# Wavelet mixing on Trainium2: the synthesis products in longer runs, and the last edge projected with its coefficients stationary

## The chip, the cores and the metric

The kernel runs on one core of a Trainium2 chip. The metric is the device time of one execution in microseconds (us); lower is better. "Before" is the kernel without the change.

## The reference, cut to what matters

```python
x: (8, 512, 207, 64) fp32               # batch, time, nodes, channels
sig = x.transpose(0, 2, 3, 1).reshape(-1, T)
a = sig; details = []
for _ in range(3):                       # 8-tap wavelet analysis along time
    a, d = _dwt(a); details.append(d)
coeffs = [a] + details[::-1]             # four components
enh = [c * w[i] for i, c in ...]         # a weight per component and channel
rec = enh[0]
for d in enh[1:]:
    rec = _idwt(rec[:, :d.shape[-1]], d)   # synthesis along time
xr = rec[:, :T].reshape(B, N, D, T).transpose(0, 3, 1, 2)
return x + xr @ proj_w.T + proj_b        # 64x64 projection of the channels
```

Analysis and synthesis are linear in time, so the kernel holds each as a small banded matrix, and it projects the channels between the two.

## The kernel before, in words

The time axis of 512 steps is cut into four windows of 128, and each window into two halves of 64 steps. Two nodes of 64 channels make a pair (128 columns of `x_sb`), four pairs make a group, and nine groups make a turn of the loop; 23 turns make 207 groups. One group is one period of the schedule. The first and last turns are written out, those between are a hardware loop. All order between engines is written by hand, with semaphores: a `wait_ge` on an engine holds everything that stands behind it on that engine.

TensorE (PE) does four kinds of work. All of it uses one half of the array's rows (64 partitions) per matmul, and two matmuls on the two halves run side by side:

- Analysis (line 433, called by `analyse_first` and `analyse_second`, L441 and L462): `x_sb` is stationary (64x128), the 84 columns of the analysis matrix move. Each pair has a first and a second piece of four matmuls. They write the two banks of `coefs_ps`; VectorE (DVE) multiplies them by the component weights into `coefs_sb` (`scale_pair`, L706). There is one `coefs_ps`, so the first piece of the next pair waits for that (`scaled`, L455). GpSimd (POOL) then adds 20 shared columns of the two halves of the time axis (`add_seam`, L364, semaphore `seamed`), which the projection of window 2 waits for.
- Projection (`project`, L487): a window's coefficients (64x128) are stationary, and the 64x64 projection weight moves. Windows go in the order 2, 3, 0, 1 (`ORDER`). Windows 2 and 0 share `proj_ps[0]`, windows 3 and 1 share `proj_ps[1]`. ScalarE (ACT) rounds the result to fp32r (`copy_high`, L634), and DVE takes the rest (`split_low`, L712); the bank is free after that (`lo_copied`).
- The tail (`project_tail`, L497): the 20 coefficient columns past the last window of time, the "last edge". Before, the weight is stationary and the coefficients move (4 pairs of 32 columns), so the result has channels on partitions. DVE turns it (`turn_tail`, L724, two transposes), ACT moves it in four pieces of 20x128 into `tail_row` (`move_tail`, L646) and rounds it into the stack (L654), and POOL takes the rest (`split_tail`, L368).
- Synthesis (L518, L520, L530, L532, and the edges L542, L544): 512 columns of fp32r move. A unit is two windows: LATE is windows 2 and 3, EARLY is windows 0 and 1. `synthesise_first` has three steps of two matmuls, `synthesise_second` three more steps and the edge step. Before, `synthesise_first` is issued as step 0, then a piece of analysis, then steps 1 and 2. DVE adds the result to `x_sb` (`add_window`, L733).

A matmul of four-byte floats shows as two records in the trace, an fp32r matmul as one. A group in TensorE's order is written in `turn_of` (L547): the two projections of windows 2 and 3 with two analysis pieces, the tail, the EARLY unit of the group two behind, then windows 0 and 1, then the LATE unit of the group one behind, and the first half of window 2 of the next group. DVE's order (`turn_of` there, its calls at the end of its block) is: add windows 2 and 3, scale pair 0, split 2, split 3, turn the tail, scale pair 1, add windows 0 and 1, scale pair 2, split 0, split 1, scale pair 3. POOL's (L393): seam 0, wait for window 3, seam 1, four DMAs, seam 2, split the tail, wait for window 1, seam 3, four DMAs. ACT's: copy 2, copy 3, an edge, move and round the tail, an edge, copy 0, copy 1, an edge. SP issues loads of `x` and stores of the output, paced by the count of analysed pairs.

Of the kernel before, what the change touches and what calls it, by code (L numbers as in the profile page):

```python
# [7 lines left out]
BATCH, TIME, NODES, CHANNELS = 8, 512, 207, 64  # L8
# [7 lines left out]
WINDOWS = TIME // WINDOW  # L16
# [8 lines left out]
QUAD = 32  # L25
# [5 lines left out]
TAIL_AT = PART_COLS + SEAM  # L31
PAIR_COLS = TAIL_AT + QUAD

# [106 lines left out]
def wavelet_mix(nc, x, comp_w, w_t, bias, analysis_m, synthesis_m, edge_m, out):  # L140
# [11 lines left out]
    with ExitStack() as ctx:  # L152
        def sb(name, shape, dtype=fp32):
            return ctx.enter_context(nc.sbuf_tensor(name, shape, dtype))
# [4 lines left out]
        def sem(name):  # L159
            return ctx.enter_context(nc.semaphore(name))  # L160
# [16 lines left out]
        bias_parts = sb("bias_parts", [1, BIAS_PARTS, GROUP], fp32r)  # L177
        coefs_sb = sb("coefs_sb", [PAIR, COEF_SETS * PAIRS, PAIR_COLS])
        proj_hi = [[sb(f"proj_hi{w}_{i}", [WINDOW, GROUP], fp32r) for i in range(SETS)] for w in range(WINDOWS)]
        proj_lo = [[sb(f"proj_lo{w}_{i}", [WINDOW, GROUP], fp32r) for i in range(SETS)] for w in range(WINDOWS)]  # L180
        tail_sb = sb("tail_sb", [4 * QUAD, PAIRS * QUAD])
        tail_row = sb("tail_row", [QUAD, GROUP])
# [31 lines left out]
        lo_copied = sem("lo_copied")  # L214
        turned = sem("turned")
        tail_moved = sem("tail_moved")
# [31 lines left out]
        def proj_of(w):  # L248
            return proj_ps[PLACE[w] % 2]
# [104 lines left out]
        def _(pool):  # L354
            nc.gpsimd.memset(stack_sb[:, EARLY * SETS:(EARLY + 1) * SETS, :].bitcast(fp32), 0.0).then_inc(stacks_cleared, 1)
            pool.wait_ge(comp_loaded, 2 * 16)
            build_scale(nc.gpsimd, 0).then_inc(scale_built, 1)

            def add_seam(turn, g, p):
                done = (turn * GROUPS + g) * PAIRS + p  # L360
                coefs = coefs_of(g, p)
                halo, own = coefs[:, SEAM:SEAM + HALO_COLS], coefs[:, PART_COLS:PART_COLS + HALO_COLS]
                pool.wait_ge(scaled, done + 1)
                nc.gpsimd.tensor_tensor(own, halo, own, ALU.add).then_inc(seamed, 1)  # L364

            def split_tail(turn, g):
# [54 lines left out]
        def _(pe):  # L421
# [49 lines left out]
            def project(turn, g, w, pairs, first):  # L471
                group = turn * GROUPS + g
                if pairs[0] == 0:
                    if w in UNITS[LATE]:
                        if not (first and g == 0):
                            pe.wait_ge(lo_copied, group * WINDOWS + (PLACE[w] - 1))
                    else:
                        pe.wait_ge(lo_copied, group * WINDOWS + (PLACE[w] - 1))
                        if w == ORDER[3]:
                            pe.wait_ge(turned, group + 1)  # L480
                for p in pairs:
# [10 lines left out]

            def project_tail(g):
                at = (g % COEF_SETS) * PAIRS
                for node in range(2):
                    rows = node_rows[node]
                    mm = nc.tensor.matmul(proj_of(ORDER[1])[:, node, NODE_COLS:NODE_COLS + PAIRS * QUAD], w_sb[rows, :],  # L497
                                          coefs_sb[rows, at:at + PAIRS, TAIL_AT:TAIL_AT + QUAD],
                                          start=True, stop=True, skip_group_check=True)
                mm.then_inc(projected, 1)  # L500
# [46 lines left out]
            def turn_of(turn, first=False, last=False):  # L547
                for g in range(GROUPS):
# [14 lines left out]

                    first_ahead(0)
                    project(turn, g, 2, [2, 3], first)
                    second_ahead(0)
                    project(turn, g, 3, [0, 1, 2, 3], first)
                    project_tail(g)
                    if with_early:
                        synthesise_first(*twice, EARLY, [0], False)  # L570
                    first_ahead(1)
                    if with_early:
                        synthesise_first(*twice, EARLY, [1, 2], False)
                    second_ahead(1)
                    if with_early:
                        synthesise_second(*twice, EARLY)
                    project(turn, g, 0, [0, 1], first)
                    first_ahead(2)
                    project(turn, g, 0, [2, 3], first)
                    second_ahead(2)  # L580
                    project(turn, g, 1, [0, 1, 2, 3], first)
                    if opening:
                        pe.wait_ge(lo_built, 2)
                        pe.wait_ge(stacks_set, 16 * STACK_DMAS)
                    if with_late:
                        synthesise_first(*behind, LATE, [0], opening)
                    first_ahead(3)
                    if with_late:
                        synthesise_first(*behind, LATE, [1, 2], opening)
                    second_ahead(3)  # L590
                    if with_late:
                        synthesise_second(*behind, LATE)
                    if not (last and g + 1 == GROUPS):
                        project(*ahead, 2, [0, 1], False)

# [4 lines left out]
            pe.wait_ge(scaled, PAIRS)  # L600
            project(0, 0, 2, [0, 1], True)
            turn_of(0, first=True)
# [8 lines left out]
        def _(act):  # L611
# [25 lines left out]
            def move_tail(turn, g, first):  # L637

                group = turn * GROUPS + g
                act.wait_ge(turned, group + 1)  # L640
                if not (first and g == 0):
                    act.wait_ge(tail_hi_copied, group)
                    act.wait_ge(tail_lo_copied, group)
                for q in range(4):
                    cols = slice(q * PAIRS * QUAD, (q + 1) * PAIRS * QUAD)
                    nc.scalar.activation(tail_row[0:HALO_COLS, cols], tail_sb[q * QUAD:q * QUAD + HALO_COLS, :],  # L646
                                         ACT.Copy).then_inc(tail_moved, 1)
# [36 lines left out]
        def _(dve):  # L684
            nc.vector.memset(warm_sb[:, :], 0.0).then_inc(warm_cleared, 1)
            nc.vector.memset(w_sb[:, :], 0.0).then_inc(cleared, 1)
            nc.vector.memset(coefs_sb[:, :, TAIL_AT + HALO_COLS:PAIR_COLS], 0.0)
            nc.vector.memset(stack_sb[:, LATE * SETS:(LATE + 1) * SETS, :].bitcast(fp32), 0.0).then_inc(stacks_cleared, 1)
# [27 lines left out]

            def turn_tail(turn, g, first):
                group = turn * GROUPS + g
                dve.wait_ge(projected, group * WINDOWS + 2)
                if not (first and g == 0):  # L720
                    dve.wait_ge(tail_moved, group * TAIL_MOVES)
                for node in range(2):
                    rows = node_rows[node]
                    last = nc.vector.transpose(tail_sb[rows, :],  # L724
                                               proj_of(ORDER[1])[rows, node, NODE_COLS:NODE_COLS + PAIRS * QUAD])
                last.then_inc(turned, 1)

            def add_window(turn, g, w):
# [6 lines left out]
            def turn_of(turn, first=False, last=False):  # L735
                for g in range(GROUPS):
# [14 lines left out]
                    split_low(turn, g, 3)  # L751
                    turn_tail(turn, g, first)
                    scale_ahead(1)
# [55 lines left out]
```

## Time and profile before

| | |
|---|---|
| median of 3 runs | 2275.58 us |
| lowest, highest | 2274.68, 2275.77 us |
| the profiled execution's own time | 2273.99 us |
| its span | 2272.1 us |
| busy share: PE, PE weight loads, DVE, ACT, POOL | 99, 95, 78, 55, 55 % |
| traffic of HBM over the span | 191 GB/s, DMA engines busy 60 to 70 % |
| groups | 207 |

The span is the stretch in which instructions ran in the profiled execution; the execution's own time is 1.9 us longer. The busy share of TensorE counts overlapping matmuls and modelled ends, so it does not say that the array works at its peak.

### The profile page before, as it was taken

The page shows a single profiled execution, that of the slowest core. Times are in us where ns is not written, and L with a number is a line of the kernel's source. Part 1 is how long each engine was busy: PE and PEld are TensorE (multiplying, and loading weights), DVE is VectorE, ACT ScalarE, POOL GpSimd, SP SyncE. Part 2 cuts the span into 40 slices and gives each one's busy share as a digit, 9 for nine tenths or more (in the row PEclk, how much of TensorE's full clock was granted, in tenths as well). Part 3 has the DMA queues.
Part 4 walks back from the last instruction along what each step waited for, and adds up shares of the span by engine and source line. Part 5 has one row for each costly group of instructions (what it writes and reads, how often), then busy time and mean ns, then how long its engine had stood idle before and what let it go on. Part 6 is the DMA issues. An engine that isn't in the chain of part 4 may idle for free.

```text
span 2272.1 us, 84681 instructions
## 1 busy us (share of the span) xinstructions
PE 2255.5 (99%) x33152; PEld 2155.0 (95%) x33152; DVE 1779.9 (78%) x2920; ACT 1248.6 (55%) x2489; POOL 1250.7 (55%) x2708
## 2 busy tenths in 40 slices
PE   9999999999999999999999999999999999999998
PEld 8999999999999999999999999999999999999997
DVE  4878777777777787777778777777777777777776
ACT  3555555555555555555555555555555555555554
POOL 3555555555555555555555555555555555555554
PEclk9999999999999999999999999999999999999999
DMA  4666767676676766767677676766767667676765
GB/s 144 211 212 217 245 213 254 210 240 222 210 250 214 249 209 215 250 210 252 208 232 234 204 255 208 249 213 214 249 210 249 213 219 241 210 256 207 247 218 174
DMA packets 165718, 507.53 MB, mean 223 GB/s; under 512 B 48710, under 2 KB 49990, under 8 KB 165403
## 3 DMA queue, kind: packets, MB, share of 16 engines
q1 hardware_dynamic: 111656, 434.23, 56.3%
q0 software_dynamic: 52992, 68.02, 12.1%
q8 instruction: 296, 4.85, 0.9%
q10 hardware_dynamic: 754, 0.28, 0.0%
q14 instruction: 20, 0.16, 0.0%
HBM read 217.33 MB, written 217.06 MB: 191 GB/s over the span
## 4 chain that ended last, share of the span: by engine, by line
PE 99%; issue 0%; DVE 0%; DMA 0%; ACT 0%; DVEq 0%; ACTq 0%
PE coefs_ps L433 33%; PE proj_ps L487 31%; PE synth_ps L518 11%; PE synth_ps L530 9%; PE synth_ps L532 4%; PE synth_ps L520 3%; PE synth_ps L542 3%; PE proj_ps L497 2%; PE synth_ps L544 1%; DVE x_sb L733 0%; DMA x_sb<-x 0%; PE proj_ps L433 0%; PE synth_ps L433 0%; DVE proj_lo L712 0%; ACT proj_hi L634 0%
## 5 line engine op out<-in xcount | busy, mean ns | idle before, releaser
L433 PE MATMUL coefs_ps<-analysis_sb,x_sb 64*128 64x84 f32 x13200 | 1029.0, 272 | 2.7 <-issue 1.9
L433 PEld LDWEIGHTS coefs_ps<-analysis_sb,x_sb 64*128 64x128 f32 x13200 | 959.5, 188 | 48.2 <-issue 3.5
L634 ACT ACTIVATE proj_hi<-proj_ps 128x512 fp32r<-128x512 f32 x828 | 494.3, 597 | 796.9 <-PE proj_ps L487 568.6
L487 PE MATMUL proj_ps<-w_sb,coefs_sb 64*128 64x64 f32 x13248 | 928.4, 268 | 2.6 <-issue 2.6
L487 PEld LDWEIGHTS proj_ps<-w_sb,coefs_sb 64*128 64x128 f32 x13248 | 896.8, 189 | 28.3 <-issue 2.8
L706 DVE TENSOR_TENSOR coefs_sb<-coefs_ps,scale_sb 128x552 f32<-128x552 f32 x825 | 604.3, 733 | 285.1 <-PE coefs_ps L433 277.6
L364 POOL TENSOR_TENSOR coefs_sb<-coefs_sb 128x20 f32<-128x20 f32 x828 | 188.1, 227 | 961.5 <-DVE coefs_sb L706 958.5
L712 DVE TENSOR_TENSOR proj_lo<-proj_ps,proj_hi 128x512 fp32r<-128x512 f32 x828 | 560.4, 688 | 137.3 <-ACT proj_hi L634 111.2
L733 DVE TENSOR_TENSOR x_sb<-synth_ps,x_sb 128x512 f32<-128x512 f32 x828 | 531.2, 683 | 56.2 <-PE synth_ps L544 56.1
L664 ACT ACTIVATE stack_sb<-proj_hi 20x512 fp32r<-20x512 f32 x621 | 387.1, 623 | 11.6
L646 ACT ACTIVATE tail_row<-tail_sb 20x128 f32<-20x128 f32 x828 | 255.3, 308 | 179.8 <-DVE tail_sb L724 164.7
L384 POOL DMA_DIRECT2D stack_sb<-proj_hi x621 | 314.0, 506 | 33.4 <-issue 31.8
L384 POOL DMA_DIRECT2D stack_sb<-proj_lo x621 | 313.9, 505 | 0.0
L368 POOL TENSOR_TENSOR tail_lo<-tail_row,stack_sb 20x512 fp32r<-20x512 f32 x207 | 263.9, 1275 | 0.1
L518 PE MATMUL synth_ps<-proj_hi,synthesis_lo 64*128 64x512 f32 x414 | 197.6, 477 | 5.2 <-DVE x_sb L733 5.2
L520 PE MATMUL synth_ps<-proj_hi,synthesis_lo 64*128 64x512 f32 x414 | 197.8, 478 | 0.0
L530 PE MATMUL synth_ps<-proj_hi,synthesis_lo 64*128 64x512 f32 x414 | 197.0, 476 | 0.3
L532 PE MATMUL synth_ps<-proj_hi,synthesis_lo 64*128 64x512 f32 x414 | 197.0, 476 | 0.0
L518 PE MATMUL synth_ps<-proj_lo,synthesis_hi 64*128 64x512 f32 x414 | 196.7, 475 | 0.0
L520 PE MATMUL synth_ps<-proj_lo,synthesis_hi 64*128 64x512 f32 x414 | 196.4, 474 | 0.0
L542 PE MATMUL synth_ps<-stack_sb,edge_all 64*128 64x512 f32 x414 | 162.3, 392 | 0.0
L530 PE MATMUL synth_ps<-proj_hi,synthesis_hi 64*128 64x512 f32 x414 | 162.2, 392 | 0.0
(57 smaller groups left out, 2716.5 us busy)
## 6 DMA issues: line engine op xcount, KB each, us to landing
x_sb<-x SPq DMA_DIRECT2D x364, 576.0 KB, 4.5
out<-x_sb SPq DMA_DIRECT2D x364, 576.0 KB, 3.5
stack_sb<-proj_hi POOLq DMA_DIRECT2D x621, 40.0 KB, 2.2
stack_sb<-proj_lo POOLq DMA_DIRECT2D x621, 40.0 KB, 3.3
stack_sb<-stack_sb POOLq DMA_DIRECT2D x207, 40.0 KB, 2.2
stack_sb<-tail_lo POOLq DMA_DIRECT2D x207, 40.0 KB, 3.3
out<-x_sb SPq DMA_DIRECT2D x1, 1280.0 KB, 4.7
x_sb<-x SPq DMA_DIRECT2D x1, 1024.0 KB, 9.3
```

Source lines behind the costliest of these rows:

```text
L384: pool.dma_start(stack_of(g, u)[rows, :].bitcast(fp32), source[0:HALO_COLS, :].bitcast(fp32)).then_inc(sent, 16)
L433: return lambda cols: nc.tensor.matmul(out[:, at:at + HALF_COLS], x_sb[half_rows[side], w, cols], analysis_sb[half_rows[side], :], start=s ...
L487: mm = nc.tensor.matmul(out_cols[:, :, p, :], coefs_of(g, p)[rows, own_cols(w)], w_sb[rows, rows].rearrange("k (h c) -> k h c", h=2), star ...
L518: nc.tensor.matmul(synth_ps[0][:, :], weight[half_rows[0], :], low[half_rows[0], :], start=step == 0, stop=False, skip_group_check=True)
L520: mm = nc.tensor.matmul(synth_ps[1][:, :], weight[half_rows[1], :], high[half_rows[1], :], start=step == 0, stop=False, skip_group_check=True)
L530: nc.tensor.matmul(synth_ps[1][:, :], weight[half_rows[0], :], high[half_rows[0], :], start=False, stop=False, skip_group_check=True)
L532: nc.tensor.matmul(synth_ps[0][:, :], weight[half_rows[1], :], low[half_rows[1], :], start=False, stop=False, skip_group_check=True)
L634: nc.scalar.activation(proj_hi[w][g % SETS][:, :].rearrange("k (n c) -> k n c", n=2), proj_of(w)[:, :, 0:NODE_COLS], ACT.Copy).then_inc(hi ...
L664: nc.scalar.activation(stack_of(g, u)[rows, :], proj_hi[w][g % SETS][0:HALO_COLS, :].bitcast(fp32), ACT.Copy).then_inc(edge_moved[w], 1)
L706: nc.vector.tensor_tensor(coefs, banks[:, :, 0:PART_COLS], scale_sb[:, :, :], ALU.mult).then_inc(scaled, 1)
L712: nc.vector.tensor_tensor(proj_lo[w][g % SETS][:, :].rearrange(by_node, n=2), proj_of(w)[:, :, 0:NODE_COLS], proj_hi[w][g % SETS][:, :].bi ...
L733: nc.vector.tensor_tensor(cols, rec, cols, ALU.add).then_inc(summed, 1)
```

## The change: what it does

TensorE's order in a group is rewritten. `synthesise_first` is issued whole, for both units. The piece of analysis that stood inside it comes after it; then come two pairs of projection; then the second piece of analysis and `synthesise_second`. To have those pairs of projection there, windows are projected in other portions: window 2 as pairs 0 and 1, pair 2, pair 3; window 3 and window 1 as pair 0 and pairs 1 to 3; window 0 as pairs 0 and 1, pair 2, pair 3.

The tail is projected like a window: GpSimd copies its 20 columns of each pair, right after the seam, side by side into a new tile `tails_sb`, that tile is stationary, and the weight moves. The result then has time on partitions, and the two DVE transposes with `tail_sb` and the semaphore `turned` are gone. ACT moves it from PSUM (four pieces as before, one for each pair), and waits for DVE's split of window 3 before it does. TensorE waits for the tail's move before it projects window 1 into the same banks.

```diff
@@ GpSimd
             pool.wait_ge(comp_loaded, 2 * 16)
+            pool.wait_ge(tails_cleared, 1)
...
                 nc.gpsimd.tensor_tensor(own, halo, own, ALU.add).then_inc(seamed, 1)
+                nc.gpsimd.tensor_copy(tails_sb[:, g % COEF_SETS, p * QUAD:p * QUAD + HALO_COLS],
+                                      coefs[:, TAIL_AT:TAIL_AT + HALO_COLS]).then_inc(tailed, 1)
@@ TensorE
                         if w == ORDER[3]:
-                            pe.wait_ge(turned, group + 1)
+                            pe.wait_ge(tail_moved, (group + 1) * TAIL_MOVES)
...
-            def project_tail(g):
-                at = (g % COEF_SETS) * PAIRS
+            def project_tail(turn, g):
+
+                i = g % COEF_SETS
+                pe.wait_ge(tailed, (turn * GROUPS + g + 1) * PAIRS)
                 for node in range(2):
                     rows = node_rows[node]
-                    mm = nc.tensor.matmul(proj_of(ORDER[1])[:, node, NODE_COLS:NODE_COLS + PAIRS * QUAD], w_sb[rows, :],
-                                          coefs_sb[rows, at:at + PAIRS, TAIL_AT:TAIL_AT + QUAD],
+                    mm = nc.tensor.matmul(proj_of(ORDER[1])[:, node, NODE_COLS:NODE_COLS + CHANNELS],
+                                          tails_sb[rows, i, :], w_sb[rows, rows],
                                           start=True, stop=True, skip_group_check=True)
...
                     first_ahead(0)
-                    project(turn, g, 2, [2, 3], first)
+                    project(turn, g, 2, [3], first)
+                    project(turn, g, 3, [0], first)
                     second_ahead(0)
-                    project(turn, g, 3, [0, 1, 2, 3], first)
-                    project_tail(g)
+                    project(turn, g, 3, [1, 2, 3], first)
+                    project_tail(turn, g)
                     if with_early:
-                        synthesise_first(*twice, EARLY, [0], False)
+                        synthesise_first(*twice, EARLY, [0, 1, 2], False)
                     first_ahead(1)
-                    if with_early:
-                        synthesise_first(*twice, EARLY, [1, 2], False)
+                    project(turn, g, 0, [0, 1], first)
                     second_ahead(1)
                     if with_early:
                         synthesise_second(*twice, EARLY)
-                    project(turn, g, 0, [0, 1], first)
+                    project(turn, g, 0, [2], first)
                     first_ahead(2)
-                    project(turn, g, 0, [2, 3], first)
+                    project(turn, g, 0, [3], first)
+                    project(turn, g, 1, [0], first)
                     second_ahead(2)
-                    project(turn, g, 1, [0, 1, 2, 3], first)
+                    project(turn, g, 1, [1, 2, 3], first)
...
                     if with_late:
-                        synthesise_first(*behind, LATE, [0], opening)
+                        synthesise_first(*behind, LATE, [0, 1, 2], opening)
                     first_ahead(3)
-                    if with_late:
-                        synthesise_first(*behind, LATE, [1, 2], opening)
+                    if not (last and g + 1 == GROUPS):
+                        project(*ahead, 2, [0, 1], False)
                     second_ahead(3)
                     if with_late:
                         synthesise_second(*behind, LATE)
                     if not (last and g + 1 == GROUPS):
-                        project(*ahead, 2, [0, 1], False)
+                        project(*ahead, 2, [2], False)
@@ ScalarE, move_tail
-                act.wait_ge(turned, group + 1)
+                act.wait_ge(lo_copied, group * WINDOWS + (PLACE[ORDER[1]] + 1))
...
-                for q in range(4):
-                    cols = slice(q * PAIRS * QUAD, (q + 1) * PAIRS * QUAD)
-                    nc.scalar.activation(tail_row[0:HALO_COLS, cols], tail_sb[q * QUAD:q * QUAD + HALO_COLS, :],
+                by_pair = tail_row[0:HALO_COLS, :].rearrange("k (n h p c) -> k n h p c", n=2, h=2, p=PAIRS)
+                for p in range(PAIRS):
+                    tail = proj_of(ORDER[1])[p * QUAD:p * QUAD + HALO_COLS, :, NODE_COLS:NODE_COLS + CHANNELS]
+                    nc.scalar.activation(by_pair[:, :, :, p, :], tail.rearrange("k n (h c) -> k n h c", h=2),
                                          ACT.Copy).then_inc(tail_moved, 1)
@@ VectorE
-            nc.vector.memset(coefs_sb[:, :, TAIL_AT + HALO_COLS:PAIR_COLS], 0.0)
+            nc.vector.memset(tails_sb[:, :, :], 0.0).then_inc(tails_cleared, 1)
...
-            def turn_tail(turn, g, first):
-                group = turn * GROUPS + g
-                dve.wait_ge(projected, group * WINDOWS + 2)
-                if not (first and g == 0):
-                    dve.wait_ge(tail_moved, group * TAIL_MOVES)
-                for node in range(2):
-                    rows = node_rows[node]
-                    last = nc.vector.transpose(tail_sb[rows, :],
-                                               proj_of(ORDER[1])[rows, node, NODE_COLS:NODE_COLS + PAIRS * QUAD])
-                last.then_inc(turned, 1)
...
                     split_low(turn, g, 3)
-                    turn_tail(turn, g, first)
                     scale_ahead(1)
```

## Rows read from the trace of the kernel before

**Rows 1.** The page: span, busy time of each engine, granted clock.

```profile
span 2272.1 us, 84681 instructions
...
PE 2255.5 (99%) x33152; PEld 2155.0 (95%) x33152; DVE 1779.9 (78%) x2920; ACT 1248.6 (55%) x2489; POOL 1250.7 (55%) x2708
...
PEclk9999999999999999999999999999999999999999
```

**Rows 2.** The page: chain that ended last, by engine.

```profile
PE 99%; issue 0%; DVE 0%; DMA 0%; ACT 0%; DVEq 0%; ACTq 0%
```

**Rows 3.** Timeline of TensorE from 1006.41 us: start, duration, line, operation, records.

```profile
1006.41 0.55 PE L487 MATMUL proj_ps<-w_sb,coefs_sb 64*128 64x64 f32 x8
1006.80 0.63 PE L433 MATMUL coefs_ps<-analysis_sb,x_sb 64*128 64x84 f32 x8
1007.27 0.59 PE L487 MATMUL proj_ps<-w_sb,coefs_sb 64*128 64x64 f32 x8
1007.70 0.63 PE L433 MATMUL coefs_ps<-analysis_sb,x_sb 64*128 64x84 f32 x8
1008.16 1.04 PE L487 MATMUL proj_ps<-w_sb,coefs_sb 64*128 64x64 f32 x16
1009.04 0.44 PE L497 MATMUL proj_ps<-coefs_sb,w_sb 64*128 64x128 f32 x4
1009.23 0.48 PE L518 MATMUL synth_ps<-proj_hi,synthesis_lo 64*128 64x512 f32 x1
...
1009.55 0.57 PE L433 MATMUL coefs_ps<-analysis_sb,x_sb 64*128 64x84 f32 x8
1009.91 0.47 PE L518 MATMUL synth_ps<-proj_lo,synthesis_hi 64*128 64x512 f32 x1
...
1010.46 0.57 PE L433 MATMUL coefs_ps<-analysis_sb,x_sb 64*128 64x84 f32 x8
1010.82 0.47 PE L530 MATMUL synth_ps<-proj_hi,synthesis_lo 64*128 64x512 f32 x1
...
1011.13 0.38 PE L530 MATMUL synth_ps<-proj_lo,synthesis_hi 64*128 64x512 f32 x1
...
1011.36 0.40 PE L530 MATMUL synth_ps<-proj_hi,synthesis_hi 64*128 64x512 f32 x1
...
1011.83 0.55 PE L487 MATMUL proj_ps<-w_sb,coefs_sb 64*128 64x64 f32 x8
1012.29 0.68 PE L433 MATMUL coefs_ps<-analysis_sb,x_sb 64*128 64x84 f32 x8
1012.80 0.60 PE L487 MATMUL proj_ps<-w_sb,coefs_sb 64*128 64x64 f32 x8
...
1013.70 1.04 PE L487 MATMUL proj_ps<-w_sb,coefs_sb 64*128 64x64 f32 x16
1014.55 0.48 PE L518 MATMUL synth_ps<-proj_hi,synthesis_lo 64*128 64x512 f32 x1
```

**Rows 4.** Timeline of VectorE in the same stretch; in brackets the idle time before.

```profile
1008.37 0.73 DVE L706 TENSOR_TENSOR coefs_sb<-coefs_ps,scale_sb 128x552 f32<-128x552 f32 x1 [0.47 <-PE coefs_ps L433]
1009.02 0.68 DVE L712 TENSOR_TENSOR proj_lo<-proj_ps,proj_hi 128x512 fp32r<-128x512 f32 x1
1010.23 0.69 DVE L712 TENSOR_TENSOR proj_lo<-proj_ps,proj_hi 128x512 fp32r<-128x512 f32 x1 [0.53 <-ACT proj_hi L634]
1010.84 0.63 DVE L724 STREAM_TRANSPOSE tail_sb<-proj_ps 64x128 f32<-64x128 f32 x2
1011.50 0.73 DVE L706 TENSOR_TENSOR coefs_sb<-coefs_ps,scale_sb 128x552 f32<-128x552 f32 x1
```

**Rows 5.** Timeline of GpSimd: a seam after the scaling that ended at 1009.10.

```profile
1009.19 0.23 POOL L364 TENSOR_TENSOR coefs_sb<-coefs_sb 128x20 f32<-128x20 f32 x1 [0.55 <-DVE coefs_sb L706]
```

**Rows 6.** The page's costliest groups: busy us, mean ns of one.

```profile
L646 ACT ACTIVATE tail_row<-tail_sb 20x128 f32<-20x128 f32 x828 | 255.3, 308 | 179.8 <-DVE tail_sb L724 164.7
...
L368 POOL TENSOR_TENSOR tail_lo<-tail_row,stack_sb 20x512 fp32r<-20x512 f32 x207 | 263.9, 1275 | 0.1
```

More of the change, by code:

```diff
@@ L31 @@
 TAIL_AT = PART_COLS + SEAM
-PAIR_COLS = TAIL_AT + QUAD
+PAIR_COLS = TAIL_AT + HALO_COLS
 PAIR = 2 * CHANNELS
@@ L178, in wavelet_mix @@
         coefs_sb = sb("coefs_sb", [PAIR, COEF_SETS * PAIRS, PAIR_COLS])
+        tails_sb = sb("tails_sb", [PAIR, COEF_SETS, PAIRS * QUAD])
         proj_hi = [[sb(f"proj_hi{w}_{i}", [WINDOW, GROUP], fp32r) for i in range(SETS)] for w in range(WINDOWS)]
         proj_lo = [[sb(f"proj_lo{w}_{i}", [WINDOW, GROUP], fp32r) for i in range(SETS)] for w in range(WINDOWS)]
-        tail_sb = sb("tail_sb", [4 * QUAD, PAIRS * QUAD])
         tail_row = sb("tail_row", [QUAD, GROUP])
@@ L214, in wavelet_mix @@
         lo_copied = sem("lo_copied")
-        turned = sem("turned")
+        tails_cleared = sem("tails_cleared")
+        tailed = sem("tailed")
         tail_moved = sem("tail_moved")
@@ L600, in _ @@
             pe.wait_ge(scaled, PAIRS)
-            project(0, 0, 2, [0, 1], True)
+            project(0, 0, 2, [0, 1, 2], True)
             turn_of(0, first=True)
```

## The prediction

> **What bounds the kernel now.** I read the page first: TensorE is busy 99% of the span at a full granted clock, VectorE 78%, the others 55% [rows 1], and the chain that ended last is TensorE's for 99% [rows 2]. So the time is what TensorE's queue takes, and I read its timeline by the distance from the start of one piece to the start of the next, not by durations, which overlap [rows 3]. One group runs from the tail at 1009.04 to the next; 207 groups follow each other. In the rows a piece of analysis (x8, four matmuls) takes 0.47 and 0.46 us where projections stand on both sides (1006.80 to 1007.27, 1007.70 to 1008.16), and 0.36 where synthesis does (1009.55, 1010.46). A half window of projection takes 0.43 after analysis, 0.39 after synthesis (1006.41 to 1006.80); a whole one 0.88 up to the tail and 0.85 up to synthesis, so one step inside is (0.88-0.43)/4 = 0.112. A pair of synthesis matmuls takes 0.23 (1011.13 to 1011.36), but the first after other work 0.32 and 0.31 (1009.23, 1010.82). The tail takes 0.19.
>
> The reader should see two things in that. Entering synthesis costs some 0.085 us. But the neighbours pay less when synthesis is beside them, because 512 moving columns cover the next weight load: 0.10 less for an analysis piece with synthesis on both sides.
>
> One place is no steady work. At 1011.83 a half window takes 0.46 where its twin at 1006.41 took 0.39, and the analysis behind it 0.51 in place of 0.465: 0.115 lost. Rows 4 say why: the analysis waits for the scaling of the pair before, which DVE started only at 1011.50, right behind the two tail transposes (1010.84); it ended at 1012.23, and TensorE went on at 1012.29. The analysis it scales had been issued by 1010.82. This place comes once in a group.
>
> **The change, part by part.**
>
> *Synthesis entries.* Before there are six a group, after four: each unit has one run of three and one of four pairs. -2 x 0.085 = -0.17.
>
> *Analysis.* Before, four pieces between synthesis and four between projections: 4 x 0.36 + 4 x 0.465 = 3.30. After, four stay between projections, two have synthesis before and projection after, two the reverse. Each kind has one of the edges that the 0.36 has two of, so the two kinds add up to 0.36 + 0.465 = 0.825 (I take 0.41 for each): 4 x 0.465 + 2 x 0.825 = 3.51. +0.21.
>
> *Projection.* Before 2 x 0.39 + 2 x 0.43 + 0.88 + 0.85 = 3.37. After: two pieces of two steps after synthesis (0.39 - 0.225 = 0.165), four half windows after analysis (0.43), and the two remainders of six steps (0.655 and 0.625): 3.33. -0.04.
>
> *The tail.* Before 0.19 up to synthesis. After it is two steps like the projection's: 0.112, and 0.085 before synthesis (a whole window is 0.03 shorter there). 0.20, so 0.00 to +0.01.
>
> The four sum to 0.00, with 0.02 either way for rounding of the rows. **The regrouping alone is worth nothing**: what two entries save, four lost covers give back.
>
> A page of the Trainium skill, "TensorE: Matmul & The Clock Gate", section "Wait — 56ns, not 53.3ns?", gives back-to-back matmuls N/2.4 ns plus about 2.5, 215.7 ns for 512 columns, and names no cost of entering. By that alone the six entries would be free and this change would cost +0.17 a group, an estimate of 2286 for the run. The rows disagree: 0.23 inside a run and 0.31 to 0.32 for its first pair, and the sum goes by them.
>
> *The transposes.* 0.63 us of DVE's work a group leaves [rows 4], and the stall of 0.115 goes if the scaling comes in time in the new order. That is the margin to work out. A scaling starts 0.67 after its analysis piece starts (1007.70 to 1008.37), takes 0.73, and counting from the stalled piece (a full-length piece ending at 1012.80 would have begun at 1012.335) TensorE can use it 0.105 later: 1.505. After the change the next analysis starts 0.41 + 1.01 (run of four, 1010.82 to 1011.83) + 0.165 = 1.585 behind. It fits with **0.08 to spare**, in both halves of the group, if DVE is free: by then it has split window 3 (ready 0.6 us before the scaling can start).
>
> *New waits.* Each is priced by what it holds, since everything behind it on TensorE stands:
> - The next group's window 2 waits for the split of window 0, now one analysis piece after the LATE run of three. Chain: 0.67, DVE's next operation starts 0.65 after the scaling's start [rows 4], split 0.68, TensorE 0.135 (a projection's second step comes 0.03 earlier than analysis's): 2.135. Available: 0.465 + 0.625 + (0.315 + 2 x 0.23 = 0.78) + 0.41 = 2.28. Spare 0.14.
> - Pair 3 of window 2 waits for seam 3: 0.67 + 0.73 + 0.09 to the seam's start + 0.23 [rows 5] + 0.135 = 1.86; available 0.41 + 1.01 + 0.165 + 0.465 = 2.05. Spare 0.19, if POOL is free.
> - POOL gets four copies of 128x20. The trace has none; between 0.23, the seam of the same shape [rows 5], and 1.275, the tail's subtraction [rows 6], I take 0.23: same shape, fewer inputs. 0.92 us more a group on an engine at 55%. The second copy delays the edges' four DMAs by up to 0.5, and their user is a group or more later. From about 0.8 per copy the chain copy, four DMAs, seam 2, copy, tail split would make seam 3 late.
> - Window 1 waits for ACT's four moves. They start after DVE's split of window 3, 1010.92 - 1009.04 = 1.88 behind the tail's start, plus 0.05; four at 0.308 [rows 6], 0.135: 3.3. Available: 0.20 + 0.78 + 0.41 + 0.43 + 0.41 + 1.01 + 0.165 + 0.465 + 0.22 = 4.09. Spare 0.8. Their source is now PSUM; bounds for one are 0.308 (same 128 elements) and 0.63, the move plus as much again. I take 0.308. ACT starts them 0.6 earlier than now, so nothing behind them is later.
> - `tailed` is set a whole group ahead. SP's loads and stores are paced by the analysis count, which shifts inside a group by less than 1 us. The one memset replaced is done while the kernel still waits for its first loads. These cost nothing.
>
> **Sum.** (0.00 - 0.115) x 207 = -23.8. The profiled execution took 2273.99, 1.6 below the median; 2273.99 - 23.8 = 2250.2 for its like, 2251.8 for the median. I take **2251**.
>
> **The rivals.**
> 1. *The margins don't hold (partly).* The scaling has 0.08 to spare, twice a group, and the split 0.14, worked out from rows rounded to 0.01. If TensorE needs its semaphore 0.1 us sooner (to load weights ahead), 2 x 0.02 a group comes back: 2259. At 0.13 it is 2 x 0.05: 2272; only past 0.137 is it more than the stall removed. For: TensorE loads weights ahead of their use. Against: the 0.105 is measured where it had just been released.
> 2. *The entries' saving stays whole.* If analysis between synthesis and projection costs no more than the 0.36, -0.21 more a group: 2251 - 43 = 2208; with half of it, 2230. Against: 0.465 and 0.36 repeat at every such place.
> 3. *Slower: the tail's move.* If one move from PSUM in its new pattern costs over 0.50, window 1 waits; from 0.53 on that outweighs the stall removed. At 0.63 the wait is 4 x 0.32 - 0.8 = 0.48, and the run 2251 + 0.48 x 207 = 2350. Against: ACT's cost follows elements per partition, 0.308 for 128.
> 4. *The change doesn't take the stall away*, as DVE is late at that point for another reason: 2275. Against: DVE's gap before the split, 0.53, shows that it isn't short of time but held in order.
>
> **How the numbers follow.** My forecast 0.72, with 2246 to 2256 as its own bounds (0.02 x 207 = 4 either way). Rival 1 0.12, rival 2 0.06, rival 3 0.05, rival 4 0.05. The range, 2243 to 2270, holds the forecast's cases and the larger part of rival 1. A measurement can tell 0.2%, 4.6 us, from no change: faster is below 2271. Faster 0.86 (forecast, rival 2, two thirds of rival 1), same 0.08, slower 0.06 (rival 3 and the last piece of rival 1).
>
> **What would show it.** In the changed trace: four first pairs of 0.31 to 0.32 a group and ten of 0.23; analysis pieces of 0.465 and about 0.41, none of 0.36; the two-step pieces after synthesis 0.165, and the analysis behind them 0.465, not 0.51; DVE idle before each scaling; the group 10.62 long in place of 10.74; ACT's moves near 0.31. I am wrong in the sum if a piece of analysis beside synthesis still takes 0.36, and wrong in the margins if the two-step piece takes over 0.165 or the analysis behind it over 0.47.

## The result, and the profile after

The changed kernel took **2337.39 us** (median of 4 runs, 2320.54 to 2351.34) beside 2275.68 us for the kernel before (4 runs, 2274.68 to 2276.86): a ratio of 1.027, interval 1.019 to 1.034. It is slower by 62 us where 2251 was forecast. The profiled execution took 2344.75 us.

The page of the changed kernel answers to [rows 1, 2, 6]:

```profile
span 2342.9 us, 84692 instructions
...
PE 2296.3 (98%) x33152; PEld 2200.0 (94%) x33152; DVE 1669.9 (71%) x2506; ACT 1215.8 (52%) x2489; POOL 1364.1 (58%) x3536
...
PEclk9999999999999999999999996999999999998998
...
q8 instruction: 296, 4.85, 0.9%
...
PE 97%; issue 2%; DVE 0%; POOL 0%; DMA 0%; ACT 0%; DVEq 0%; POOLq 0%; ACTq 0%
...
L654 ACT ACTIVATE tail_row<-proj_ps 20x128 f32<-20x128 f32 x828 | 222.6, 269 | 66.8 <-DVE proj_lo L720 51.7
```

VectorE went from 78% to 71%, as its transposes left. ScalarE's move from PSUM takes 269 ns, less than the 308 of [rows 6]. No other engine came onto the chain. What is new is 2% of "issue" in the chain, and single slices of the clock row in which it is not full (6 in one, 8 in two).

One group in the middle of the run, TensorE's timeline (start, duration; the second matmul of each synthesis pair is left out):

```profile
1083.46 0.47 PE L524 MATMUL synth_ps<-proj_hi,synthesis_lo 64*128 64x512 f32 x1
...
1083.77 0.39 PE L524 MATMUL synth_ps<-proj_lo,synthesis_hi 64*128 64x512 f32 x1
...
1084.00 0.39 PE L524 MATMUL synth_ps<-proj_hi,synthesis_hi 64*128 64x512 f32 x1
...
1084.23 0.59 PE L437 MATMUL coefs_ps<-analysis_sb,x_sb 64*128 64x84 f32 x8
1084.64 0.61 PE L491 MATMUL proj_ps<-w_sb,coefs_sb 64*128 64x64 f32 x8
1085.07 0.65 PE L437 MATMUL coefs_ps<-analysis_sb,x_sb 64*128 64x84 f32 x8
1085.49 0.48 PE L536 MATMUL synth_ps<-proj_hi,synthesis_lo 64*128 64x512 f32 x1
...
1086.50 0.35 PE L491 MATMUL proj_ps<-w_sb,coefs_sb 64*128 64x64 f32 x4
1086.67 0.65 PE L437 MATMUL coefs_ps<-analysis_sb,x_sb 64*128 64x84 f32 x8
1087.13 0.61 PE L491 MATMUL proj_ps<-w_sb,coefs_sb 64*128 64x64 f32 x8
...
1093.88 0.41 PE L503 MATMUL proj_ps<-w_sb,tails_sb 64*128 64x64 f32 x4
1094.07 0.47 PE L524 MATMUL synth_ps<-proj_hi,synthesis_lo 64*128 64x512 f32 x1
```

Little is wrong here. The group takes 1094.07 - 1083.46 = 10.61 us; 10.62 was forecast. The first synthesis pair takes 0.31, those behind it 0.23; analysis between synthesis and projection 0.41 and 0.42; the two-step piece 0.17 (1086.50 to 1086.67), and the analysis behind it 0.46, so the stall is gone. VectorE waits for TensorE before its scaling, no longer the other way round:

```profile
1085.75 0.73 DVE L714 TENSOR_TENSOR coefs_sb<-coefs_ps,scale_sb 128x552 f32<-128x552 f32 x1 [0.65 <-PE coefs_ps L437]
...
1090.94 0.73 DVE L714 TENSOR_TENSOR coefs_sb<-coefs_ps,scale_sb 128x552 f32<-128x552 f32 x1 [0.72 <-PE coefs_ps L437]
```

The loss is elsewhere. The view of waits names 19 on TensorE's analysis that it puts down to no other engine (us in total, times, longest):

```profile
PE coefs_ps L437 <- issue: 31.1, 19, 2.5
```

All of them stand at the loop's back edge: between the two-step projection that ends a turn of nine groups and the first analysis of the next turn. The loop makes 21 passes, so its closing branch is taken 20 times and once falls through. One of them in the timeline, and the stretches around it (length, busy us of each engine, granted clock, DMA share, GB/s):

```profile
2117.67 0.39 PE L548 MATMUL synth_ps<-stack_sb,edge_all 64*128 64x512 f32 x1
...
2117.91 0.34 PE L491 MATMUL proj_ps<-w_sb,coefs_sb 64*128 64x64 f32 x4
2120.72 1.15 PE L437 MATMUL coefs_ps<-analysis_sb,x_sb 64*128 64x84 f32 x8 [2.47 <-issue]
2121.65 1.04 PE L491 MATMUL proj_ps<-w_sb,coefs_sb 64*128 64x64 f32 x8
```

```profile
2110.00:2117.90 7.90, 7.90 (x116) 7.51 (x114) 5.89 (x9) 5.25 (x11) 4.20 (x11) 1.00 0.67 206
2117.90:2120.70 2.80, 0.35 (x6) 0.20 (x2) 1.29 (x2) 0.00 (x0) 2.30 (x6) 0.91 0.21 44
2120.70:2140.00 19.30, 19.28 (x154) 18.25 (x156) 6.80 (x10) 5.85 (x12) 4.47 (x13) 0.50 0.14 47
2141.00:2151.00 10.00, 10.00 (x156) 9.43 (x154) 7.62 (x12) 5.86 (x12) 5.33 (x14) 1.00 0.66 214
```

The next analysis comes 2.64 us later than the 0.17 us of a two-step piece would let it (2120.72 in place of 2118.08), and then TensorE works at a granted clock of 0.50, the lower of its two levels (1.2 GHz), for 19 us: 154 matmul records there, 156 in the 10 us after. Not every gap is followed by this: of the 19, of 0.75 to 2.47 us, nine were, for 6.8 to 37.5 us. Added up over the packed trace, the 20 back edges are 34 us late, and 156.6 us were granted half the clock, 20 of them at the very end of the run, where the kernel before has 10.6 too.

From the ninth group on, 198 groups took 2200.2 us here and 2103.7 with the same work and another place of the loop's head (below): 96.5 more, of which 34 are the late back edges. That leaves 62 to the half clock. An estimate agrees: the window above loses some 9.4 us in 19.3, and 136 us at that rate, the half clock inside this stretch, are 67.

What TensorE waits for shows in the records of the line that closes the loop (count, duration ns least/median/most, first and last start; the 22 are one on entering, 20 taken, one on leaving). Kernel before:

```profile
L603 PEldq COMPARE_BRANCH  x22: 88/858/1570, 122.9 to 2159.5; - x22
```

and after:

```profile
L610 PEldq COMPARE_BRANCH  x22: 87/2680/3747, 123.6 to 2224.2; - x22
```

### The profile page after: what moved, and what is told of

Same layout as the page of the kernel before. It is cut to its first block, busy times and chain, and to the rows that moved or that the text cites. A ratio compares the mean times of both kernels' runs of the same rounds, so it can differ in the third digit from the quotient of the medians.

```text
span 2342.9 us, 84692 instructions
## 1 busy us (share of the span) xinstructions
PE 2296.3 (98%) x33152; PEld 2200.0 (94%) x33152; DVE 1669.9 (71%) x2506; ACT 1215.8 (52%) x2489; POOL 1364.1 (58%) x3536
## 3 DMA queue, kind: packets, MB, share of 16 engines
q8 instruction: 296, 4.85, 0.9%
## 4 chain that ended last, share of the span: by engine, by line
PE 97%; issue 2%; DVE 0%; POOL 0%; DMA 0%; ACT 0%; DVEq 0%; POOLq 0%; ACTq 0%
PE coefs_ps L437 33%; PE proj_ps L491 31%; PE synth_ps L524 12%; PE synth_ps L536 12%; PE synth_ps L548 4%; PE proj_ps L503 2%; PE synth_ps L526 1%; PE synth_ps L538 1%; PE synth_ps L550 0%; DVE x_sb L730 0%; DVE coefs_sb L714 0%; DMA x_sb<-x 0%; PE proj_ps L437 0%; POOL stack_sb L388 0%; POOL tail_lo L372 0%
## 5 line engine op out<-in xcount | busy, mean ns | idle before, releaser
L437 PE MATMUL coefs_ps<-analysis_sb,x_sb 64*128 64x84 f32 x13200 | 1070.8, 279 | 32.7 <-issue 31.1
L491 PE MATMUL proj_ps<-w_sb,coefs_sb 64*128 64x64 f32 x13248 | 1020.8, 271 | 3.4 <-issue 1.9
L491 PEld LDWEIGHTS proj_ps<-w_sb,coefs_sb 64*128 64x128 f32 x13248 | 964.7, 193 | 28.7 <-issue 2.5
L654 ACT ACTIVATE tail_row<-proj_ps 20x128 f32<-20x128 f32 x828 | 222.6, 269 | 66.8 <-DVE proj_lo L720 51.7
L524 PE MATMUL synth_ps<-proj_hi,synthesis_lo 64*128 64x512 f32 x414 | 201.3, 486 | 4.4 <-DVE x_sb L730 4.4
L536 PE MATMUL synth_ps<-proj_hi,synthesis_lo 64*128 64x512 f32 x414 | 202.8, 490 | 0.2
L538 PE MATMUL synth_ps<-proj_hi,synthesis_lo 64*128 64x512 f32 x414 | 202.8, 490 | 0.0
L526 PE MATMUL synth_ps<-proj_hi,synthesis_lo 64*128 64x512 f32 x414 | 201.4, 486 | 0.0
L536 PE MATMUL synth_ps<-proj_lo,synthesis_hi 64*128 64x512 f32 x414 | 166.8, 403 | 0.0
L538 PE MATMUL synth_ps<-proj_lo,synthesis_hi 64*128 64x512 f32 x414 | 166.7, 403 | 0.0
L548 PE MATMUL synth_ps<-stack_sb,edge_all 64*128 64x512 f32 x414 | 165.8, 400 | 0.0
L550 PE MATMUL synth_ps<-stack_sb,edge_all 64*128 64x512 f32 x414 | 165.8, 400 | 0.0
```

What stands on the lines that cost most here:

```text
L437: return lambda cols: nc.tensor.matmul(out[:, at:at + HALF_COLS], x_sb[half_rows[side], w, cols], analysis_sb[half_rows[side], :], start=s ...
L491: mm = nc.tensor.matmul(out_cols[:, :, p, :], coefs_of(g, p)[rows, own_cols(w)], w_sb[rows, rows].rearrange("k (h c) -> k h c", h=2), star ...
L524: nc.tensor.matmul(synth_ps[0][:, :], weight[half_rows[0], :], low[half_rows[0], :], start=step == 0, stop=False, skip_group_check=True)
L536: nc.tensor.matmul(synth_ps[1][:, :], weight[half_rows[0], :], high[half_rows[0], :], start=False, stop=False, skip_group_check=True)
L538: nc.tensor.matmul(synth_ps[0][:, :], weight[half_rows[1], :], low[half_rows[1], :], start=False, stop=False, skip_group_check=True)
```

## The experiments

Each ratio is against the kernel before on the same chip. All the variants compute the whole reference.

**Is it the instruction fetch?** Three kernels: the change with another place of the loop's head, and its two parts alone.

Head at place 16 (branch at 227 of its block):

```diff
-LOOP_SLOT = 144
+LOOP_SLOT = 16
```

> The changed kernel with the loop's first TensorE instruction at slot 16 of its fetch block in place of 144; nothing else differs. The body is 3027 instructions in both kernels, so the closing branch then stands 227 instructions into its block in place of 99. Theory A (the fetch of the loop's head is asked for when TensorE's queue enters its last block, and in the new order that is too late): the gap at the back edge of 1.6 us and the clock drops behind it go, 2235 to 2245 us. Theory B (the fetch is late because data transfers stand before it): the slot does nothing, 2320 to 2350. Theory C (the new order lowers the clock by itself, without the gaps): about 2330 with a clock near 0.97.

Measured 2250.2 us (2244.79 to 2253.45), ratio 0.989 (0.987 to 0.991). The branch, and a back edge in the timeline:

```profile
L610 PEldq COMPARE_BRANCH  x22: 88/357/2232, 123.2 to 2128.8; - x22
```

```profile
698.50 0.35 PE L491 MATMUL proj_ps<-w_sb,coefs_sb 64*128 64x64 f32 x4
698.67 0.65 PE L437 MATMUL coefs_ps<-analysis_sb,x_sb 64*128 64x84 f32 x8
699.13 0.62 PE L491 MATMUL proj_ps<-w_sb,coefs_sb 64*128 64x64 f32 x8
```

No gap, 0.17 as inside a turn; 6.4 us at half clock in the whole run. One constant, which touches no work, gives back 87 us; Theory A came true but for 5 us. The loss is the late instruction fetch at the back edge, with the clock that falls behind it, and the rest of the change does what was forecast.

The tail alone, with TensorE's `turn_of` of the kernel before and place 144:

```diff
...
-                        synthesise_first(*behind, LATE, [0, 1, 2], opening)
+                        synthesise_first(*behind, LATE, [0], opening)
                     first_ahead(3)
-                    if not (last and g + 1 == GROUPS):
-                        project(*ahead, 2, [0, 1], False)
+                    if with_late:
+                        synthesise_first(*behind, LATE, [1, 2], opening)
...
```

> The change's tail alone (coefficients stationary, copies by GpSimd, no transposes) in TensorE's order of before. If the late fetch comes from TensorE's order: the group falls from 10.74 to 10.62 as the 0.115 us stall behind the transposes goes, back edges as before, 2248 to 2254 us. If it comes from GpSimd's added copies (its DMAs issued later, into the time of the fetch): gaps of over 1 us at the back edges and over 2300.

The new order alone, tail and transposes as before, place 144 (the reverse edit of `turn_of` on the kernel before):

> TensorE's new order alone, with the tail and the two transposes as before. If the late fetch comes from the order: gaps of over 1 us at the back edges, over 2310 us; the groups between at 10.60 to 10.65, since the transposes stand ahead of a scaling that now has time. If from the tail's part: 2240 to 2255.

The tail alone: 2253.6 us (2250.31 to 2256.29), 0.990 (0.989 to 0.992), its branch 0.88 us. The order alone: 2329.45 us (2315.47 to 2335.96), 1.023 (1.019 to 1.028):

```profile
L604 PEldq COMPARE_BRANCH  x22: 88/2840/3380, 123.2 to 2207.3; - x22
```

So the **order** makes the branch late, not the tail, and not GpSimd's four copies, which this kernel does not have. Its groups inside a turn take 10.60 to 10.61 us, and 123.7 us ran at half clock.

**Is the fetch late because data transfers stand in its way?** Every load and store of SyncE was paced one analysed pair earlier, so that the last packets of `x` and `out` end some 3 us before the branch (the median end in the changed kernel is at the branch):

```diff
-                at = s * 2 * SLOT_DMAS + 4 * PAIRS + 2 + (SLOT_DMAS if loading else 0)
+                at = s * 2 * SLOT_DMAS + 4 * PAIRS + 1 + (SLOT_DMAS if loading else 0)
```

> The changed kernel with every load and store of SyncE paced one analysed pair (2.65 us) earlier; the last load ahead of the back edge is then out of the way before the fetch. Theory B (data transfers delay the fetch): the fetch comes 0.7 us or more earlier, most of the gap goes, 2240 to 2280 us. Theory A (the place of the branch in its block decides): 2320 to 2350 as it was.

2350.6 us (2317.43 to 2362.93), 1.035 (1.030 to 1.039). The branch took 2.66 us in the median and the fetch started 0.38 us after it: no earlier. SyncE's transfers are not what holds it.

**How does the place act?** Place 176 (branch at 131) on the changed kernel:

> The changed kernel with the loop's first instruction at slot 176, so that the closing branch stands 131 instructions into its block (99 as changed, 227 in e1). 32 instructions are about 1 us of the queue. If the fetch simply follows the entry into the last block, it comes about 1 us earlier, from a mean near 0.3 us behind the branch to 0.7 before it, the gap shrinks from 1.6 to about 0.6 us and most clock drops go: 2265 to 2300 us. If it is held up by something in a fixed place behind which it now falls or not (GpSimd's burst of edge transfers 2 to 0.5 us ahead of the branch), it jumps by 2 us or more: 2245 to 2260 us.

2268.51 us (10 runs, 2259.49 to 2287.3), 0.999 (0.996 to 1.001). The fetch came 1.84 us earlier, not the 1 us that 32 instructions take. The branch took 0.87 us and 18 of 20 back edges are clean (the other two 0.4 us late), but the time is not that of place 16. The timeline shows why:

```profile
606.05 0.84 PE L491 MATMUL proj_ps<-w_sb,coefs_sb 64*128 64x64 f32 x12
606.70 0.91 PE L503 MATMUL proj_ps<-w_sb,tails_sb 64*128 64x64 f32 x4
607.43 0.49 PE L524 MATMUL synth_ps<-proj_hi,synthesis_lo 64*128 64x512 f32 x1
```

```profile
PE proj_ps L503 <- issue: 5.2, 12, 0.9
```

The tail of a turn's first group takes 0.73 to the next piece in place of 0.19. It stands 80 instructions behind the head, and a head at place 176 leaves exactly 80 in its block: the second block is late now. A turn's first group took 11.35 us in the median where the others took 10.59 to 10.62, and 20 times that difference is 15 of the 18 us to place 16.

The kernel before, at place 128 (branch at 83) and at place 16:

> The kernel before with the loop's first instruction at slot 128: the closing branch 83 instructions into its block in place of 99. If the slot of before only just held, half a microsecond less lead costs 0.4 us more at each of 21 back edges and some clock drops: 2284 to 2310 us. If before has room, it stays at 2276.

> The kernel before with the loop's first instruction at slot 16. Its back edges lose about 0.19 us each in the trace of before; with the fetch 5 us ahead that is gone: 2276 - 4 = 2272 us, 2269 to 2274. The stall behind the transposes stays, groups of 10.74.

Place 128 took 2274.73 us (1.000, interval 0.999 to 1.001), the second of the two cases; place 16 took 2276.16 us (1.001, 1.000 to 1.002), a miss. At 128 half a microsecond less lead did not make the branch longer:

```profile
L603 PEldq COMPARE_BRANCH  x22: 88/666/2139, 121.8 to 2158.4; - x22
```

One of the 20 taken ones came late by 1.4 us (the 2139 ns), and 3.4 us at half clock followed. At 16 the fetch starts 7.0 us ahead, and all the middle turns take 96.73 to 96.77 us (10.75 a group) where they took 96.7 to 97.6, so the gain at the back edges is there, some 5 us. It is lost at the loop's two ends:

```profile
125.76 0.68 PE L433 MATMUL coefs_ps<-analysis_sb,x_sb 64*128 64x84 f32 x8 [1.44 <-issue]
...
2161.42 0.21 PE L487 MATMUL proj_ps<-w_sb,coefs_sb 64*128 64x64 f32 x1 [1.40 <-issue]
```

The first gap stands where the loop is entered (that branch took 2.44 us, 0.20 at place 144), the second some 30 instructions behind its exit, where the branch's block ends, and 3.4 and 6.8 us at half clock follow. Counted from the tail of one turn's ninth group to the next turn's, these two turns took 99.83 and 101.02 us where the kernel before took 96.69 and 96.04: 3.1 and 5.0 us more. The kernel before had nothing to win from this constant.

**What is each part worth with the fetch out of the way?** The tail alone and the order alone, both at place 16:

> The tail's part alone with the loop's first instruction at slot 16. By my sum the regrouping is worth nothing and the transposes all of the gain, so this should equal e1 within 3 us: 2246 to 2252 us. If the fewer synthesis entries are worth something after all, it is slower than e1 by 5 us or more.

> The new order alone (tail and transposes as before) with the loop's first instruction at slot 16. With the gaps gone, groups of 10.61 us as in e3 between its back edges: the transposes don't delay a scaling in this order either. 2248 to 2254 us. If the order needs the tail's part to gain, it stays at 2265 or above.

2248.54 us (0.989, 0.987 to 0.991) and 2249.74 us (0.992, 0.989 to 0.994), beside 0.989 (0.987 to 0.991) for both parts together. Groups are 10.60 to 10.62 us in all three. Each part removes the same stall, and the two do not add. Four entries to synthesis in place of six are worth nothing that the run times can tell. In the traces a turn takes 95.44 us with both parts and 95.63 with the tail alone: 0.02 us a group, 4 us a run, as much as the runs of one kernel differ among themselves.

**Where in the turn does the order act?** The change, place 144, with only the last LATE half of each turn in the old order, about the last 100 instructions of 3027 (42 matmul and 42 weight-load records and some ten waits):

```diff
+                    closing = g + 1 == GROUPS and not last
...
-                        synthesise_first(*behind, LATE, [0, 1, 2], opening)
+                        synthesise_first(*behind, LATE, [0] if closing else [0, 1, 2], opening)
                     first_ahead(3)
-                    if not (last and g + 1 == GROUPS):
+                    if closing:
+                        synthesise_first(*behind, LATE, [1, 2], opening)
+                    elif not last or g + 1 < GROUPS:
                         project(*ahead, 2, [0, 1], False)
...
+                    if closing:
+                        project(*ahead, 2, [0, 1, 2], False)
+                    elif not last or g + 1 < GROUPS:
                         project(*ahead, 2, [2], False)
```

> The changed kernel, slot 144, but the last LATE half of each turn in the order of before: step 0, analysis, steps 1 and 2, analysis, second part, and window 2 of the next group behind it (pairs 0 to 2). Some 110 instructions ahead of the closing branch differ, and nothing else. If the order of these sets when the head is fetched: the fetch is back at 1.8 us ahead of the branch, no gap over 0.3 us on average, 2246 to 2256 us. If the order of the whole turn does: gaps as in the changed kernel, 2310 or more.

2255.46 us (10 runs, 2248.57 to 2283.18), 0.994 (0.991 to 0.997):

```profile
L615 PEldq COMPARE_BRANCH  x22: 88/949/2312, 123.4 to 2135.5; - x22
```

The fetch starts 1.49 us ahead again, and 3.6 us ran at half clock in the profiled execution, which was the fastest of the ten. The loss hangs on the last 100 instructions of a turn.

**The worst and the best place.** Place 48 puts the branch 3 instructions into its block; place 0 puts it at 211.

> The changed kernel with the loop's first instruction at slot 48: the closing branch 3 instructions into its block. If the fetch waits for the entry into the last block, it comes at the branch or behind it, some 3 us after the queue has run over, at every back edge: gaps of 1.6 to 2.5 us, 2330 to 2390 us. If nothing ties it to the block, as e1 or as changed.

> The changed kernel with the loop's first instruction at slot 0: the branch 211 instructions into its block and a whole block ahead of the second one. As e1 within 3 us, 2246 to 2253; below that if something of the slot still costs in e1.

Place 48: 2427.24 us (2 runs, 2411.82 and 2442.67), 1.068 (1.061 to 1.076), beyond what was expected; the clock was halved for 275 us:

```profile
PEclk9998979999999999989999999999999999898998
...
PE 97%; issue 2%; DVE 0%; POOL 0%; ACT 0%; DVEq 0%; POOLq 0%; ACTq 0%
```

```profile
L610 PEldq COMPARE_BRANCH  x22: 88/3362/3682, 123.3 to 2295.4; - x22
```

Place 0: **2245.72 us** (2243.91 to 2248.35), 0.988 (0.987 to 0.990), the fastest, though not told apart from place 16, and faster than both kernels:

```profile
L610 PEldq COMPARE_BRANCH  x22: 88/452/2395, 124.4 to 2130.3; - x22
```

The five places of the changed kernel in one table (medians; the start of the head's fetch is counted from the branch):

| head at | branch at | fetch starts, us | branch takes, us | time, us |
|---|---|---|---|---|
| 48 | 3 | +1.0 | 3.36 | 2427.24 |
| 144 | 99 | +0.32 | 2.68 | 2337.39 |
| 176 | 131 | -1.5 | 0.87 | 2268.51 |
| 0 | 211 | -4.2 | 0.45 | 2245.72 |
| 16 | 227 | -6.4 | 0.36 | 2250.2 |

The places vary two things at once: at 0 and 16 a turn also spans 12 blocks, at the other three 13. The five runs do not part the branch's place from that.

## Why the prediction was wrong

**The step that failed** is the sum's last one, "(0.00 - 0.115) x 207". It gives every group the saving of a group in the middle of a turn, and puts nothing on the 20 places where one turn of the loop follows another. There the closing branch and the fetch of the loop's head stand on TensorE's queue, and neither the parts nor the rivals name them. The change reorders what stands ahead of that branch, so this was an unpriced part of it. The view "one line's instructions" of the kernel before already had the number: a branch of 0.86 us in the median, 1.57 at most, and 0.27 more to the analysis, over a cover of 1.08. There was no margin left, and the branch grew by 1.8 us in the median. The price: 34 us of late back edges and 62 us with the lower clock, against a saving of some 25.

**The rivals.** None of the four happened. The slower one, the tail's move from PSUM, was wrong in its price: 269 ns, not over 500. A forecast of slower needed a rival that was not there: a fetch later than its cover, which costs from a branch of about 1.2 us on (1.44 less 0.27).

**What held.** With the fetch moved ahead by the constant alone, the same work takes 2250.2 us or 2245.7; 2251 was forecast.
- *The four terms of regrouping* sum to 0.00: shown within the stated 0.02 by the tail alone, which keeps six entries and takes 10.62 a group beside 10.60. The measured pieces are 0.31 for a first pair, 0.41 and 0.42 for analysis with synthesis on one side, 0.17 for two steps, 0.19 to 0.20 for the tail.
- *The stall* was sized right, 10.74 to 10.61 us a group. Its cause was told only in half: the transposes ahead of the scaling make it, and it goes without them, but in the new order it also goes with them still there, as it seems because the next analysis is issued later. The prediction took the saving once, so the sum stands.
- *The new waits* all fitted their margins: VectorE stood idle 0.65 and 0.72 us before the scalings, and the split never held TensorE, the seam's wait 1.2 us in the whole run. GpSimd's copy takes 200 ns, 230 was taken.
- *The formula without a cost of entering*, N / 2.4 ns plus about 2.5 from the Trainium skill, "TensorE: Matmul & The Clock Gate", section "Wait — 56ns, not 53.3ns?", would have taken away the 0.17 a group that two entries save: an estimate. The first pair's 0.31 beside 0.23 says no here as in [rows 3].

**What stays open.** Why the new order starts the fetch 2 us later than the old one, with the branch at the same place of its block, isn't settled. It is set by the last 100 instructions of a turn, and neither SyncE's transfers nor GpSimd's copies make it. In all 14 traces the fetch starts behind the queue's entry into the block that holds the branch, never ahead of it, by 0.25 us at least and 4.0 at most. What differs is that delay: in the median 1.3 us in the kernel before, 3.2 in the changed one, 1.7 with the last half in the old order, 0.8 and 2.4 at places 16 and 0. Whether the edge transfers that GpSimd issues in the same microseconds make it was not tried. In the run with SyncE paced earlier their last packet ended 0.58 us before the branch in the median, in place of 0.36 behind it, and the fetch came no earlier, which speaks against their packets. No run leaves out the BRANCH_PREFETCH_HINT, so its part is open too. Nor does the fetch move in proportion to the place: from 99 to 131, 32 instructions, it gains 1.84 us, while from 3 to 99 it gains 0.69.

## What to carry to other kernels

Price a hardware loop's back edge like any other wait whenever instructions near the loop's end are reordered: read the closing branch's duration from its line, add what follows up to the first matmul, and set it against the work that the queue still holds when the branch starts. If the margin is a few tenths of a microsecond or less, measure the change at two or three places of the loop's head before judging it; here one constant separates 1.068, 1.027 and 0.988 of the time before. And before counting on fewer switches between kinds of matmuls, count the weight loads that lose their cover.

## What the runs showed of the hardware that was not expected

- **A gap can cost twice.** A gap of 2.5 us on TensorE was followed by some 20 us at a granted clock of 0.50, one of 1.2 us by 7. Of 19 gaps in the changed kernel nine were followed by it; one of 2.1 us was not. Over the run 34 us of late back edges came with 156.6 us at half clock, and at place 48 the clock was halved for 275 us.
- **Late fetches come at the second block too.** A head with 80 instructions left in its block had a nearly clean back edge and then lost about 0.5 to 0.8 us where the next block begins.
- **The fetch of the head can start before or after the branch**, from 7.0 us ahead to 1.0 behind in the median, by the head's place and by what the last instructions of the turn are. The loop's first instruction ran 2.7 and 2.5 us after the fetch's start in the kernels before and after.
- **Entering and leaving the loop** cost 3.1 and 5.0 us more, with the half clock that followed, when the head's place was moved from 144 to 16 in the kernel before.
